# A relational graph layer on one core: 15 whole tiles and the ends of 5 others are fetched by SyncE instead of GpSimd

## What is computed

```python
seg = edge_dst * 40 + edge_type
S   = segment_sum(h[edge_src], seg, num_segments=n * 40).reshape(n, 40, 128)
cnt = segment_sum(ones(edge_src.shape), seg, num_segments=n * 40).reshape(n, 40)
agg = einsum('nrd,rdf->nf', S, relation_weights) + cnt @ rFeatures
h   = agg * norm                         # norm = max(degree, 1) ** -0.5
h   = relu(h + h @ loop_weight)
out = layernorm(x + h)
```

## Time and profile before

| | |
|---|---|
| median of 3 runs | 1070.57 us (1070.49 to 1072.32) |
| profiled execution, first to last instruction (span) | 1067.5 us |
| between the span and the median | 3.1 us |
| busy PE / PEld / DVE / ACT / POOL | 89 / 80 / 69 / 50 / 74% of the span |
| granted TensorE clock, mean | 0.990 of full speed |
| DMA issues by SP for `BY_ROW` rows | 1162 |
| gathers by POOL, from `x` / from `x_parts` | 85 / 736 |

### The profile page before, as it was taken

One profiled execution on the slowest core, in us unless ns is written; L12 is line 12 of the kernel. 1 busy time (PEld: TensorE's weight loads), 2 busy tenths in 40 slices (PEclk: granted clock), 3 DMA queues, 4 the chain that ended last, 5 costly groups with the idle time before them and its releaser, 6 DMA issues.

```text
span 1067.5 us, 28985 instructions
## 1 busy us (share of the span) xinstructions
PE 954.3 (89%) x6713; PEld 852.9 (80%) x6713; DVE 741.5 (69%) x2588; ACT 531.6 (50%) x1137; POOL 789.4 (74%) x836
## 2 busy tenths in 40 slices
PE   2589999998999999999988999999899999999997
PEld 0378888887888888888878888888788888888887
DVE  6698877666767676667667666766667676767673
ACT  1576655444454454545454454455445544544551
POOL 7777777777777777777777777777777777777770
PEclk9799999999999999999999999999999999999999
DMA  5952334434333333434434434333333334333330
GB/s 165 296 190 56 89 110 118 115 113 118 114 113 115 116 115 115 115 114 118 115 114 115 117 112 116 113 112 112 115 112 112 113 111 115 112 112 112 114 110 24
DMA packets 64548, 125.18 MB, mean 117 GB/s; under 512 B 16835, under 2 KB 36006, under 8 KB 64374
## 3 DMA queue, kind: packets, MB, share of 16 engines
q0 software_dynamic: 38048, 102.09, 33.3%
q1 hardware_dynamic: 12294, 14.85, 4.2%
q10 hardware_dynamic: 14032, 6.35, 2.0%
HBM read 113.62 MB, written 9.60 MB: 115 GB/s over the span
## 4 chain that ended last, share of the span: by engine, by line
PE 45%; DMA 27%; POOL 13%; issue 8%; DVE 1%; POOLq 0%; ACT 0%; ACTq 0%; DVEq 0%; SPq 0%
DMA rows<-x_parts,src 27%; PE win_ps L1003 23%; PE agg_ps L1015 19%; POOL rows L505 13%; PE win_ps L1088 1%; PE win_ps L1041 1%; PE win_ps L992 1%; POOL raw L512 1%; DMA x_in<-x 0%; PE win_ps L1040 0%; POOLq L504 0%; DMA raw<-x,src 0%; ACT ring L595 0%; POOLq L117 0%; DVE ring L897 0%
## 5 line engine op out<-in xcount | busy, mean ns | idle before, releaser
L505 POOL DMA_INDIRECT rows<-x_parts,src x736 | 698.2, 949 | 224.3 <-issue 153.9
L595 ACT COPY ring<-win_ps 128x451 f32 x831 | 465.2, 560 | 362.9 <-PE win_ps L1003 206.7
L1003 PE MATMUL win_ps<-hot,rows 128*128 128x480 f32 x1642 | 563.1, 428 | 71.7 <-DMA rows<-x_parts,src 64.6
L1015 PEld LDWEIGHTS agg_ps<-ring,w 128*128 128x128 f32 x3936 | 551.2, 191 | 40.9
L1015 PE MATMUL agg_ps<-ring,w 128*128 128x128 f32 x3936 | 559.5, 274 | 0.0
L795 DVE TENSOR_SCALAR hot<-iota,key_f 128x480 fp32r<-128x480 f16 x831 | 392.6, 473 | 0.8 <-issue 0.8
L897 DVE TENSOR_TENSOR ring<-ring,win_ps 128x41 f32 x831 | 188.0, 226 | 293.7 <-DMA rows<-x_parts,src 234.3
L1003 PEld LDWEIGHTS win_ps<-hot,rows 128*128 128x128 f32 x1642 | 252.7, 192 | 114.8 <-DMA rows<-x_parts,src 103.4
L512 POOL DMA_INDIRECT raw<-x,src x85 | 89.3, 1051 | 25.9 <-issue 20.7
L992 PEld LDWEIGHTS win_ps<-hot_node,hot_type 128*128 128x128 bf16 x831 | 79.7, 99 | 33.3 <-issue 15.1
L992 PE MATMUL win_ps<-hot_node,hot_type 128*128 128x12 bf16 x831 | 85.4, 170 | 21.0 <-DVE ring L897 12.7
(11 more groups left out here) (87 smaller groups left out, 259.5 us busy)
## 6 DMA issues: line engine op xcount, KB each, us to landing
x_out<-x_parts SPq DMA_DIRECT2D x1162, 1.0 KB
rows<-x_parts,src POOLq DMA_INDIRECT x736
x_parts<-x_out SPq DMA_DIRECT2D x12, 512.0 KB, 3.3
x_in<-x SPq DMA_DIRECT2D x12, 256.0 KB, 4.4
out<-out_sb ACTq DMA_DIRECT2D x48, 64.0 KB
x_blk<-x ACTq DMA_DIRECT2D x47, 64.0 KB
w<-relation_w SPq DMA_DIRECT2D x8, 320.0 KB
raw<-x,src POOLq DMA_INDIRECT x85
```

The source lines that it names most:

```text
L505: pool.indirect_dma_start(rows[0:n, k].rearrange("p c d -> p (c d)").bitcast(F32), None, x_parts, bass.IndirectOffsetOnAxis(ap=src[0:n, t: ...
L595: nc.scalar.copy(ring[:, :, bass.ds(start + 1, WIN - 1)], win_ps[bank_of(t)][:, :, 1:WIN]).then_inc(copied, 1)
L1003: ins = nc.tensor.matmul(banks[bank_of(t)][:, 0:R * WIN], of[:, part], hot[:, t % HOTS], start=False, stop=(part == PARTS - 1), skip_group ...
L1015: ins = nc.tensor.matmul(sums_of(c), w[:, r, :], ring[:, r, bass.ds(seg, BLOCK)], start=(r == 0), stop=(r == COLS - 1))
```

## The change

The list `BY_ROW` gets 20 entries: whole tiles in blocks 7, 10, 13, ..., 46 and the last tile of ten rows (15), and five tiles that both engines fetch (`POOL_PART`): of the middle tiles of blocks 9, 18, 27, 36 and 45 POOL gathers the first 126, 124, 127, 112 and 64 rows, and SP the other 2, 4, 1, 16 and 64. All of SP's indices are loaded at the start into a tensor of their own, one tile to a partition; DVE multiplies them by 1024 once, and SP uses the products as byte offsets into a byte view of `x_parts`.

```diff
-BY_ROW = [i * TPB + TPB // 2 for i in range(7, BLOCKS - 1, 5)] + [-(-E // P) - 1]
+POOL_PART = {9: 126, 18: 124, 27: 127, 36: 112, 45: 64}
+BY_ROW = [i * TPB + TPB // 2 for i in sorted([*range(7, BLOCKS - 1, 3), *POOL_PART])] + [-(-E // P) - 1]
+BY_BOTH = {i * TPB + TPB // 2: n for i, n in POOL_PART.items()}
+ROW_BYTES = 2 * D * 4
...
-        by_row_src = x_in[0:1].rearrange("o h n d -> o (h n) d").bitcast(I32)
+        by_row_src = sb("by_row_src", [len(BY_ROW), P], I32)
+        by_row_at = sb("by_row_at", [len(BY_ROW), P], I32)
+        x_bytes = x_parts.bitcast(U8).rearrange("n b -> (n b)").unsqueeze(0)
...
+        def first_by_row(t):
+            return BY_BOTH.get(t, 0)
+        def gathers_through(t):
+            return t + 1 - len([n for n in BY_ROW if n <= t and n not in BY_BOTH])
...
             sp.dma_start(w[0:R, R, :], r_features).then_inc(w_loaded, 16)
+            sp.wait_ge(by_row_cleared, 1)
+            for j, t in enumerate(BY_ROW):
+                of = src_by_tile[t:t + 1, :] if t < FULL else src_rest.rearrange("p o -> o p")
+                sp.dma_start(by_row_src[j:j + 1, 0:rows_in_tile(t)], of).then_inc(by_row_src_loaded, 16)
             sp.wait_ge(pos_done, 1)
...
-                for j in range(BY_ROW_BUFS):
-                    load_by_row_src(j)
                 index = [sp.alloc_register(f"sp_row{n}") for n in range(ROW_LOAD)]
+                sp.wait_ge(by_row_ready, 1)
                 for j, t in enumerate(BY_ROW):
-                    sp.wait_ge(by_row_src_loaded[j], 16)
                     if j >= BY_ROW_BUFS:
                         sp.wait_ge(tile_done, BY_ROW[j - BY_ROW_BUFS] + 1)
-                    for p in range(rows_in_tile(t)):
-                        if p % ROW_LOAD == 0:
-                            n = min(ROW_LOAD, rows_in_tile(t) - p)
-                            sp.load(index[0:n], by_row_src[0:1, j % BY_ROW_BUFS, p:p + n])
-                        row = sp.snap(index[p % ROW_LOAD], min_val=0, max_val=N - 1)
-                        sp.dma_start(by_row[p:p + 1, j % BY_ROW_BUFS].rearrange("p c d -> p (c d)").bitcast(F32),
-                                     x_parts[bass.ds(row, 1), :]).then_inc(by_row_landed[j], 16)
-                    if j + BY_ROW_BUFS < len(BY_ROW):
-                        load_by_row_src(j + BY_ROW_BUFS)
+                    for n, p in enumerate(range(first_by_row(t), rows_in_tile(t))):
+                        if n % ROW_LOAD == 0:
+                            m = min(ROW_LOAD, rows_in_tile(t) - p)
+                            sp.load(index[0:m], by_row_at[j:j + 1, p:p + m])
+                        at = sp.snap(index[n % ROW_LOAD])
+                        sp.dma_start(by_row[p:p + 1, j % BY_ROW_BUFS].rearrange("p c d -> p (c d)").bitcast(U8),
+                                     x_bytes[:, bass.ds(at, ROW_BYTES)]).then_inc(by_row_landed[j], 16)
...
             def gather(t):
+                if t in BY_BOTH:
+                    j, n = BY_ROW.index(t), BY_BOTH[t]
+                    if j >= BY_ROW_BUFS:
+                        pool.wait_ge(tile_done, BY_ROW[j - BY_ROW_BUFS] + 1)
+                    pool.indirect_dma_start(
+                        by_row[0:n, j % BY_ROW_BUFS].rearrange("p c d -> p (c d)").bitcast(F32), None, x_parts,
+                        bass.IndirectOffsetOnAxis(ap=src[0:n, t:t + 1], axis=0), engine_sem=gather_issued).then_inc(
+                            both_landed[t], 16)
+                    return
...
+            nc.vector.memset(by_row_src[:], 0).then_inc(by_row_cleared, 1)
             nc.vector.memset(zeros[:], 0.0).then_inc(zeros_done, 1)
...
-                        dve.wait_ge(gather_issued, last + 1 - len([n for n in BY_ROW if n <= last]))
+                        dve.wait_ge(gather_issued, gathers_through(last))
...
                 for j in range(LOW_AHEAD):
                     low(0, j)
+                dve.wait_ge(by_row_src_loaded, len(BY_ROW) * 16)
+                nc.vector.tensor_scalar(by_row_at[:], by_row_src[:], float(ROW_BYTES), None, ALU.mult).then_inc(by_row_ready, 1)
                 dve.wait_ge(pos_ready, 16)
...
-                        pe.wait_ge(by_row_landed[BY_ROW.index(t)], rows_in_tile(t) * 16)
+                        pe.wait_ge(by_row_landed[BY_ROW.index(t)], (rows_in_tile(t) - first_by_row(t)) * 16)
+                        if t in BY_BOTH:
+                            pe.wait_ge(both_landed[t], 16)
```

More of the change, by code:

```diff
@@ L11 @@
 I32 = mybir.dt.int32
+U8 = mybir.dt.uint8
 F32R = mybir.dt.float32r
@@ L266, in build @@
         gather_issued = sem("gather_issued")
-        by_row_src_loaded = [sem(f"by_row_src_loaded{j}") for j in range(len(BY_ROW))]
+        by_row_cleared = sem("by_row_cleared")
+        by_row_src_loaded = sem("by_row_src_loaded")
+        by_row_ready = sem("by_row_ready")
+        both_landed = {t: sem(f"both_landed{t}") for t in BY_BOTH}
         by_row_landed = [sem(f"by_row_landed{j}") for j in range(len(BY_ROW))]
```

## The result

1068.13 us, median of 10 runs (1066.12 to 1068.65), against 1070.63 for the kernel before on the same chip (10 runs): ratio 0.9974, 95% interval 0.9964 to 0.9983. The change is faster, by 2.5 us by the medians (2.8 by the ratio) where 6.3 were forecast. The measured time is inside the stated range of 1062.8 to 1068.5, near its upper end.

A forecast was written before the change was run, and what follows sets the result against it. POOL, issuing gathers without a hole, was taken as the bound. Five fewer save 6.3 us, other terms 0: span 1067.5 - 6.3 = 1061.2, and the median 3.1 above it, 1064.3 us; range 1062.8 to 1068.5.

The forecast's parts named there:

- the bound: POOL issues gathers without a hole from 118 to 1040 us, one every 1.2535 us; the other engines follow.
- the worth of a skipped gather: On POOL from 118 us on: five gathers fewer at 1.2535 us each save 6.27 us.
- SP: SP's queue must issue 1879 rows in 912.7 us, 0.486 us a row; cost at the end 0, up to 3 us.
- The nearest row: SP's address instruction: a 44 ns FUSED_REGOPS becomes a MOVE as on ACT, making a row 15 to 20 ns shorter.
- The first rival: SP becomes the bound: a row still costs 0.506 us and PE waits before tile 790; 1099 us, chance 0.10.
- the start: Before the first gathers: 20 index loads hide in SP's wait for pos_done, DVE's extra work in its idle time; cost 0.
- I take 0: POOL's five shortened gathers cost what whole ones do, as bytes have no influence; -0.65 and +1.8 us kept for the range.
- rival 3: At block 27 a gather of 127 rows lands on one engine, PE 6.8 us behind; 1071.1 us if POOL is held, chance 0.04.
- being late costs nothing: SP's rows a few us late at block 46: POOL is not stopped for 16 us, PE makes good 3.7 us.
- two of the signs that the prediction had named for being wrong: PE waiting over 5 us before tile 790 or at tile 467 (127 rows); POOL's shortened gathers over 1.3 us.
- Rival 4: PE or DVE bounds once POOL skips more, giving back up to the whole gain: 1068.5 to 1070.6 us, chance 0.05.
- SP's rows being late: SP 4 to 10 us late at 0.488 to 0.491 us a row: 1066.5 to 1070.6 us, chance 0.08.

The follow-up runs named there:

- none shared: The changed kernel with POOL_PART emptied, so 15 whole tiles and no tile fetched by both engines: 1064.17 us, ratio 0.9949 to the kernel before.
- the kernel without the wait: 15 whole tiles, no tile fetched by both engines, DVE's add no longer waiting until POOL issued the gather five tiles on: 1099.37 us, ratio 1.0235 to before.

## Why the prediction was right or wrong, step by step

**Right: the bound, and the worth of a skipped gather.** The kernel with none shared measured it: 1064.17 us for 1064.3, by the ratio 5.5 us gained (3.9 to 7.1) for 6.3, and the last gather at 1033.35 for 1033.0. The 3.1 us between span and median hold 1.2 us of scatter: in each run that lists both, the time is 1.8 to 1.9 us over the span. That does not touch the forecast of the gain.

**Right: SP.** The nearest row (a MOVE for the FUSED_REGOPS) was the right one; a row came 29 ns shorter (0.506 - 0.477), not 20, and the tile of block 46 was there some 12 us before PE took it, not on the microsecond. SP started its rows at 75.6 and not at 74.1, which the shorter row more than made good. The first rival did not come true here. Its mechanism was seen on the slow chip, where a row took 0.82 us and the kernel with 15 whole tiles needed 1665 us against 1390.7:

```profile
PE win_ps L1027 <- DMA x_out<-x_parts: 333.6, 13, 29.9
```

**Right: the start.** Twenty loads on SP from 6.3 to 12.2 us, inside its wait for pos_done; DVE's multiplication took 0.21 us and lay under DVE's idle time.

**Wrong: "I take 0" for the five shortened gathers.** They took 0.99, 1.30, 2.55, 0.93 and 0.91 us where 0.95 each stood: +1.9 us in sum, a little over the end of +1.8 kept for the range. The reasoning went from bytes (which do not matter) to rows (which do, if the divisor is small). The rule was in the text, from the Trainium skill, "DMA: Bandwidth & Descriptors", section "Why a DMA increments its semaphore by 16 and not by 1"; the trace agrees with it, by POOL's times above and by the landings (10.3 us with 127 rows, 5.0 with 124, 2.7 with 112). I had priced what it does to the landing and not what it does to the instruction on the engine that bounds the kernel.

**Wrong: rival 3's price, and "being late costs nothing".** The tile of 127 rows landed 10.3 us after its issue and PE stood 5.2 us. With that and the gather of 2.55 us, two of the signs that the prediction had named for being wrong came about. Half of the argument held: POOL was not stopped, and PE, busy without a gap from 607.5 to 640, made the time good. But two things were left out. PE's first products behind its wait, from the timeline, and then the stretches around them in the changed kernel:

```profile
601.32 1.14 PE L1027 MATMUL win_ps<-hot,x_out 128*128 128x480 f32 x2 [5.21 <-DMA x_out<-x_parts,src]
...
590.00:600.00 10.00, 6.12 (x49) 5.70 (x47) 7.39 (x21) 3.73 (x8) 7.86 (x8) 1.00 0.34 92
600.00:607.50 7.50, 6.18 (x25) 5.73 (x26) 1.51 (x6) 1.25 (x3) 5.93 (x6) 0.54 0.39 115
607.50:620.00 12.50, 12.50 (x96) 11.71 (x95) 9.31 (x33) 6.68 (x15) 9.49 (x10) 1.00 0.41 114
620.00:640.00 20.00, 20.00 (x153) 18.78 (x152) 15.50 (x56) 11.84 (x25) 15.12 (x17) 1.00 0.40 113
```

TensorE, idle for 5 us, was granted 0.54 of its clock in the next 7.5 us, so some 7 of them at its lower level, 1.2 GHz, and the two matmuls of a tile took 1.14 us there instead of 0.68; that adds to the lag. And while PE, ACT and DVE caught up, DVE was out of step with POOL, whose gathers grew by up to 0.23 us each, 1.4 us in all. On an engine that bounds the kernel this is lost for good. That DVE's place in time makes the length of the gathers is shown by the kernel without the wait; which of the two neighbouring DVE instructions holds POOL, and on what, no run here shows. The Trainium skill, "DMA: Bandwidth & Descriptors", section "SWDGE vs HWDGE vs iDMA", says that GpSimd writes its descriptors to memory that VectorE locks it out of in one of its modes; the 999 ns against 949 point the same way, but no run here looks at the mode. Rival 3 saw the end result only by way of POOL "held", with a chance of 0.04: its mechanism came true, and the end result in part, at 2 to 3 us instead of 6.8, by longer gathers and not by a POOL that waits.

**Rival 4** (PE or DVE bounds) did not show: with 15 whole tiles the gain was within its interval of the full worth. With 16 it stays open.

**Luck: the range.** The 1068.13 us lie inside it only because it had been drawn up to 1068.5 for SP's rows being late. They were early; what filled that room was another cost.

## What to carry to other kernels

When a gather on GpSimd is shortened, leave it a number of rows that 16 divides; a gather of 127 rows took 1.6 us more than one of 128, and landed over 7 us later than one of 112. Before costing an instruction on the bounding engine at nothing, ask what its shape does there, and test one that is odd. And a lag that is "made good" is free only if catching up does not slow the engine that bounds.

## What had not been expected of the hardware

- The gather's time on POOL follows the number of rows on one engine: 0.93 us with 7, 0.99 with 9, 1.20 with 25, 1.29 with 31, 1.81 with 59, 2.55 with 127.
- A wait that only keeps DVE in step with POOL is worth 31 us in 1064: gathers of 949 ns on average with it, 999 without.
- A gather takes 1.14 us on average instead of 0.95 when DVE starts the making of `hot` 0.05 to 0.25 us ahead of it (kernel without the wait).
- The making of `hot` that began 0.8 us into the gather of 127 rows of the change took 1.97 us instead of 0.46 and ended 0.2 us behind that gather. This was seen once; behind the other gathers of 127 rows DVE had waited for their issue.
- A stall of PE of 5.2 us brought TensorE's lower clock for some 7 us.
- One chip ran the kernel before in 1390.7 us, and there the list of 15 whole tiles is 20% slower than before with its list of ten. The change's worth hangs on SP's pace, which is not the same on every chip.
